# Chunk 0 of a feed-forward on one core: activations handled in TensorE's order, the down weights split earlier, and the sum T1 kept in a buffer of its own

## The reference

```python
x = x + xattn(layernorm(x), ctx, mask)       # one head, 257 context rows per batch
x = x + attn(layernorm(x), Wq, Wk, Wv, Wo)   # 16 heads of 64, causal over 32
n = layernorm(x)                             # feed-forward, hidden width 4096
x = x + (silu(n @ w_gate.T) * (n @ w_up.T)) @ w_down.T
```

## Time and profile before

| | us |
|---|---|
| median of 3 runs | 1522.84 (1522.38 to 1523.93) |
| the profiled execution | 1522.65 |
| its span | 1520.9 |
| TensorE busy | 1494.1 |
| VectorE / ScalarE / GpSimd busy | 786.9 / 539.9 / 859.4 |
| mean granted clock of TensorE | 0.996 |

### The profile page before, as it was taken

One profiled execution on the slowest core, in us unless ns is written; L12 is line 12 of the kernel. 1 busy time (PEld: TensorE's weight loads), 2 busy tenths in 40 slices (PEclk: granted clock), 3 DMA queues, 4 the chain that ended last, 5 costly groups with the idle time before them and its releaser, 6 DMA issues.

```text
span 1520.9 us, 23259 instructions
## 1 busy us (share of the span) xinstructions
PE 1494.1 (98%) x8012; PEld 1208.3 (79%) x8012; DVE 786.9 (52%) x1245; ACT 539.9 (35%) x1089; POOL 859.4 (57%) x701
## 2 busy tenths in 40 slices
PE   7999999999999999999999999999999999999998
PEld 5666788888888888778888888888888888888886
DVE  5776336154162396846436436436436446446346
ACT  3335323132132243333433433433333433433342
POOL 1111221211302221588798798798798798797795
PEclk9999999999999999999999999999999999999999
DMA  9772310100101000021121121121121121121122
GB/s 366 282 291 113 134 56 29 56 28 28 55 28 55 29 1 22 8 77 49 41 76 44 46 76 36 53 75 35 56 71 34 54 76 34 55 76 34 55 62 110
DMA packets 41798, 110.38 MB, mean 73 GB/s; under 512 B 4672, under 2 KB 4800, under 8 KB 39328
## 3 DMA queue, kind: packets, MB, share of 16 engines
q1 hardware_dynamic: 41328, 109.07, 21.0%
q10 hardware_dynamic: 432, 0.79, 0.2%
HBM read 105.65 MB, written 4.19 MB: 72 GB/s over the span
## 4 chain that ended last, share of the span: by engine, by line
PE 91%; DVE 5%; issue 1%; ACT 1%; DMA 1%; SPq 0%; DVEq 0%
PE ps L1249 37%; PE ps L1269 18%; PE ps L900 9%; PE ps L901 8%; PE ps L902 8%; PE ps L934 3%; PE ps L976 2%; PE ps L952 2%; PE ps L906 1%; DVE t_raw L1598 1%; PE ps L1050 1%; PE ps L1093 1%; DMA ctx<-in_ctx 1%; DVE x L1681 1%; DVE x L1584 1%
## 5 line engine op out<-in xcount | busy, mean ns | idle before, releaser
L536 POOL TENSOR_TENSOR b_lo<-blk,b_hi 128x512 fp32r<-128x512 f32 x180 | 239.5, 1339 | 53.2 <-ACT b_hi L795 45.0
L463 POOL TENSOR_TENSOR w_lo<-raw,w_hi 128x2048 fp32r<-128x2048 f32 x16 | 74.5, 4655 | 300.9 <-ACT w_hi L649 300.9
L1681 DVE TENSOR_TENSOR x<-ps,x 128x1024 f32<-128x1024 f32 x210 | 242.1, 1208 | 0.0
L1249 PE MATMUL ps<-xT_hi,b_hi 128*128 128x512 f32 x480 | 187.0, 390 | 2.2 <-DVE x L1584 2.2
L1249 PE MATMUL ps<-xT_hi,b_lo 128*128 128x512 f32 x480 | 186.8, 389 | 0.0
L1249 PE MATMUL ps<-xT_lo,b_hi 128*128 128x512 f32 x480 | 186.8, 389 | 0.0
L1269 PE MATMUL ps<-b_hi,b_hi 128*128 128x512 f32 x420 | 166.4, 396 | 0.0
L1269 PE MATMUL ps<-b_lo,b_hi 128*128 128x512 f32 x420 | 163.8, 390 | 0.0
L1269 PE MATMUL ps<-b_hi,b_lo 128*128 128x512 f32 x420 | 163.7, 390 | 0.0
L1655 DVE TENSOR_TENSOR hid<-ps,kept 128x512 f32<-128x512 f32 x60 | 41.5, 691 | 229.6 <-PE ps L1249 189.7
L536 POOL TENSOR_TENSOR b_lo<-s_sum,b_hi 128x512 fp32r<-128x512 f32 x105 | 138.4, 1318 | 30.5 <-ACT b_hi L795 30.5
(11 more groups left out here) (166 smaller groups left out, 3232.1 us busy)
## 6 DMA issues: line engine op xcount, KB each, us to landing
blk<-in_blocks SPq DMA_DIRECT2D x180, 256.0 KB, 2.7
ctx<-in_ctx SPq DMA_DIRECT2D x64, 512.0 KB, 8.7
raw<-in_w SPq DMA_DIRECT2D x19, 1024.0 KB, 4.9
x<-in_x SPq DMA_DIRECT2D x8, 512.0 KB, 4.8
out<-x SPq DMA_DIRECT2D x16, 256.0 KB, 2.6
xn<-in_ext ACTq DMA_DIRECT2D x3, 128.0 KB, 6.6
mask<-in_mask ACTq DMA_DIRECT2D x1, 257.0 KB, 8.4
extT<-in_ext_t ACTq DMA_DIRECT2D x1, 128.0 KB, 3.8
```

Of the source, the lines that this page charges most:

```text
L463: pool.tensor_tensor(w_lo[wslot][:, :], raw[slot][:, :], w_hi[wslot][:, :].bitcast(F32), ALU.subtract).then_inc(split_done[slot], 1)
L536: pool.tensor_tensor(b_lo[slot][:, :], src[:, :], b_hi[slot][:, :].bitcast(F32), ALU.subtract).then_inc(block_lo, 1)
L1249: mm = pe.matmul(ps[:, bank, :], stat[a], moving[b], start=first and m == 0, stop=(s == 3 and m == 2), skip_group_check=True)
L1681: dve.tensor_tensor(part, ps[:, bank:bank + 2, :], part, ALU.add).then_inc(down_added, 1)
```

## The change

Three things. On ScalarE the high part of the down weights is taken right behind that of the second gate/up weights, before the turn of token tile 6. On ScalarE and VectorE the hidden parts are handled in the order 0, 2, 1, 3 (`FIRST_HIDDEN` holds for each part its place in it, and is its own inverse), with the low part of one taken later than its product, and `down` waits for two low parts instead of three. T1 gets a buffer of its own in `raw3`, is begun before the third gate/up pair ends, and goes ahead of T2 in the order of high and low parts; the additions stand in fewer and longer pieces. The first block of chunk 1 lies on `raw3`, so ScalarE waits for T1's low part before it.

```diff
-        t1_top = sb_at("t1_top", "xT_hi1", 0, [P, K4])
-        t1_raw = sb_at("t1_raw", "xT_lo1", 0, [P, K4])
+        t1_raw = sb_at("t1_raw", "raw3", 0, [P, K4])
...
+        FIRST_HIDDEN = (0, 2, 1, 3)
...
             pair_split(NG - 1, 5)
+            weights(2, ATT_USES, 2)
             turned_hi(2, NT - 2)
...
-                act.wait_ge(gu_done, 3 if n == 1 else n + 1)
+                count = FIRST_HIDDEN.index(n) + 1
+                act.wait_ge(gu_done, count)
                 act.activation(sg(half), ps[:, 2 * n, :], ACT.Silu).then_inc(silu_done, 1)
-                act.wait_ge(h_done, n + 1)
+                act.wait_ge(h_done, count)
...
             first_hidden(0)
+            first_hidden(2)
             turned_sum_hi(1, t3_hi[:, :], raw[1][:, :])
             first_hidden(1)
-            weights(2, ATT_USES, 2)
-            first_hidden(2)
-            turned_sum_hi(2, w_hi[0][:, :], t2_raw[:, :])
             first_hidden(3)
+            turned_sum_hi(2, flat(xT_hi[1][:, 0:4, :]), t1_raw[:, :])
+            turned_sum_hi(3, w_hi[0][:, :], t2_raw[:, :])
+            act.wait_ge(t_ready, 2)
             block_high(1, 0)
             block_high(1, 1)
-            turned_sum_hi(3, flat(xT_hi[1][:, 0:4, :]), t1_raw[:, :])
+            turned_sum_hi(4, w_hi[1][:, :], t4_raw[:, :])
             act.wait_ge(split_done[2], ATT_USES + 1)
             block_high(1, 2)
             block_high(1, 3)
-            turned_sum_hi(4, w_hi[1][:, :], t4_raw[:, :])
...
-                        pe.wait_ge(h_ready, c * 4 + 3)
+                        pe.wait_ge(h_ready, c * 4 + 2)
...
-                        pe.wait_ge(h_done, c * 4 + (i // 2 + 1))
+                        pe.wait_ge(h_done, c * 4 + (FIRST_HIDDEN.index(i // 2) + 1))
...
-                dve.wait_ge(silu_done, n + 1)
+                dve.wait_ge(silu_done, FIRST_HIDDEN.index(n) + 1)
+                if n >= 2:
+                    dve.wait_ge(h_ready, FIRST_HIDDEN.index(n - 2) + 1)
                 dve.tensor_tensor(gf(half), sg(half), ps[:, 2 * n + 1, :], ALU.mult).then_inc(h_done, 1)
-                dve.wait_ge(h_hi_done, n + 1)
+
+            def first_hidden_lo(n):
+                k, half = n // 2, n % 2
+                cols = slice(half * HALF, (half + 1) * HALF)
+                dve.wait_ge(h_hi_done, FIRST_HIDDEN.index(n) + 1)
                 dve.tensor_tensor(h_lo[:, k, cols], gf(half), h_hi[:, k, cols].bitcast(F32),
                                   ALU.subtract).then_inc(h_ready, 1)
```

More of the change, by code:

```diff
@@ L1614, in _ @@
             combine(raw[0][:, :], b22[0], b12[0], ALU.subtract)
+            first_hidden_lo(0)
+            first_hidden(2)
             combine(raw[1][:, :], b22[1], b12[1], ALU.subtract)
+            first_hidden_lo(2)
             combined()
             combine(raw[1][:, :], raw[1][:, :], raw[0][:, :], ALU.add, raw=True)
-            first_hidden(1)
+            dve.wait_ge(split_done[3], ATT_USES)
+            combine(t1_raw[:, :], b12[0], b11[0], ALU.subtract)
             dve.wait_ge(gu_done, 3)
@@ L1621, in _ @@
             combine(t2_raw[:, :], raw[1][:, :], b11[0], ALU.add)
+            first_hidden(1)
+            turned_sum_lo(1, t3_lo[:, :], raw[1][:, :], t3_hi[:, :])
+            first_hidden_lo(1)
             combined()
+            combine(t1_raw[:, :], t1_raw[:, :], b12[1], ALU.add)
+            combined()
+            combine(t1_raw[:, :], t1_raw[:, :], b11[1], ALU.subtract, raw=True)
             combine(t2_raw[:, :], t2_raw[:, :], b11[1], ALU.add, raw=True)
-            first_hidden(2)
-            turned_sum_lo(1, t3_lo[:, :], raw[1][:, :], t3_hi[:, :])
             first_hidden(3)
-            combine(t1_top[:, :], b12[0], b11[0], ALU.subtract)
-            first_add(0, 2)
-            combine(t1_raw[:, :], b12[1], b11[1], ALU.subtract)
-            first_add(2, 4)
-            combined()
-            combine(t1_raw[:, :], t1_raw[:, :], t1_top[:, :], ALU.add, raw=True)
-            first_add(4, 7)
-            turned_sum_lo(3, flat(xT_lo[1][:, 0:4, :]), t1_raw[:, :], flat(xT_hi[1][:, 0:4, :]))
-            first_add(7, 10)
-            combine(t4_raw[:, :], b21[0], t2_raw[:, :], ALU.subtract)
-            first_add(10, 13)
+            dve.wait_ge(t_raw, 3)
+            combine(t4_raw[:, :], b21[0], t2_raw[:, :], ALU.subtract)
+            first_hidden_lo(3)
+            turned_sum_lo(2, flat(xT_lo[1][:, 0:4, :]), t1_raw[:, :], flat(xT_hi[1][:, 0:4, :]))
+            first_add(0, 5)
+            turned_sum_lo(3, w_lo[0][:, :], t2_raw[:, :], w_hi[0][:, :])
+            first_add(5, 10)
             combined()
             combine(t4_raw[:, :], t4_raw[:, :], b21[1], ALU.add, raw=True)
-            first_add(13, 16)
-            turned_sum_lo(2, w_lo[0][:, :], t2_raw[:, :], w_hi[0][:, :])
+            first_add(10, 16)
             turned_sum_lo(4, w_lo[1][:, :], t4_raw[:, :], w_hi[1][:, :])
```

## The result

| | before | after |
|---|---|---|
| median, us | 1522.84 (1522.29 to 1523.93, 6 runs) | 1516.88 (1515.56 to 1518.41, 6 runs) |
| profiled execution / its span | 1522.65 / 1520.9 | 1518.41 / 1516.6 |

The ratio is 0.9961, with a 95% interval of 0.9948 to 0.9974: **faster by 5.96 us**. The forecast was 7.0 saved and 1515.8. The median lies 1.1 above it and inside the range.

A forecast was written before the change was run, and what follows sets the result against it. TensorE, busy 98%, bounds the kernel; only its stalls and slow clock can be won. Stall terms of -2.92 - 1.44 - 0.71 - 0.11 - 1.77 - 0.08 = -7.0 us take the median from 1522.84 to 1515.8; range 1515.0 to 1518.6.

The forecast's parts named there:

- VectorE's queue: Chunk 0 into chunk 1: VectorE's operations timed one by one from 613.4, with all 16 additions done at 646.9.
- The split at no cost: Down weights' split moved to GpSimd at 593.2 to 597.8: taken at 0, at most 1.9 us if uncovered.
- The room ahead of place 0: Start of chunk 1: 13th addition at 645.0, TensorE needs it at 645.87, so 0.8 us of room.
- the second rival: GpSimd still runs the split across T1's sums, VectorE 4.3 later: 3.5 us lost, 1519.3; chance 0.01.
- The first rival: At the start of chunk 1 a part returns as a wait for VectorE's additions: 1516.7 to 1519.7; chance 0.09.
- the slower rival: ScalarE's `b_hi2` waits behind T4's copy in a loop through four engines: 1526.1 if 14.5 late; chance 0.04.
- The sum of the stalls: TensorE, 624 to 656: 2.92 + 1.44 + 0.71 + 0.11 + 1.77 + 0.08 = 7.03 us, all removed.
- the slow clock's term: TensorE behind the first stall, 626.98 to 630.46: nine intervals at the lower clock cost 1.44 us more.
- the ceiling of 7.03: Most the change can give, from TensorE's intervals; taken over the 7.17 by which place 1 moves.
- from 656 on the program is the same: Everything behind the turn from chunk 0 to chunk 1 is untouched, so no gain or loss there.
- The sign that I had named for it: If the stalls go and the span does not follow, something behind 656 absorbs it and the untouched-rest claim fails.

The follow-up runs named there:

- run 4: The changed kernel with the down weights' split left late: 1519.64 us, 2.8 slower than the change.
- run 6: The kernel before with one more long-met ScalarE wait ahead of the chunk loop (103 instructions): 1523.65 us, ratio 1.0007.
- run 3: The kernel before with only the hidden parts reordered, split late and T1 as before: 1521.39 us, ratio 0.9992.
- run 2: The kernel before with only the down weights' split moved ahead: 1518.28 us, ratio 0.9975.
- run 7: The kernel before with the split moved ahead and the hidden parts reordered, T1 as before: 1518.81 us, ratio 0.9975.
- run 1: The changed kernel measured a second time, unaltered: 1516.82 us, ratio 0.9964.
- run 5: The changed kernel without ScalarE's wait for `split_done[2]`, 102 instructions ahead of the loop again: 1515.23 us, ratio 0.9951.
- run 10: The changed kernel with one more long-met ScalarE wait, 104 instructions ahead of the loop: 1515.72 us, ratio 0.9951.

## Why the prediction was right, and where it was not

The forecast held in sign, in place and nearly in size. Taken step by step:

- **VectorE's queue: right.** The prediction's ends against after's rows less 1.54: T1's first subtraction starts at 609.20 (609.3), T2's first half at 613.38 (613.4), T1's second sum at 619.00 (619.1), the down matmuls at 624.06 (624.06), place 0 at 645.82 (645.87), place 1 at 648.54 (648.60). The durations came from other instances of the same shape in before.
- **The split at no cost: right.** It starts at 594.62, 1.54 earlier is 593.08, and takes 4.61; nothing waits for it.
- **The room ahead of place 0: too small.** The 13th addition ended at 643.88 + 1.88 = 645.76, 1.6 ahead of 647.36 instead of 0.8. Half of the difference was there before T2 low (additions 0 to 4 ended at 634.40, less 1.54, where I had 634.8: pitches rounded up), and GpSimd held T2 low for 0.6 (2.90 against 2.29) instead of 0.85. T4's second half wasn't held (2.28), as argued. It cost nothing here, but it mis-priced the second rival: 3.5 lost, where run 4 lost 2.8. The first rival, a wait for additions, didn't come: TensorE has no wait there in after.
- **ScalarE's queue, the slower rival: rightly small.** `b_lo2` ran from 646.50, ended at 647.79, less 1.54 is 646.25, where I had 647.1.
- **The sum of the stalls: nearly right as a total, wrong in its parts.** From 626.98 to 630.46 there are eight intervals and not nine, so the slow clock's term was 3.48 - 8 x 0.227 = 1.66 instead of 1.44, and the ceiling of 7.03 that I took as "the smaller" was 7.25. Run 6 agrees: without that term, and with 0.08 behind the stall, its down matmuls end 1.60 earlier. I also wrote the terms as if each stall had a cause of its own. Run 6 removes the slow clock's term and place 1 doesn't move; run 3 removes 2.92 + 1.66 and only 1.2 comes. All three are one chain: VectorE is late, its additions with it, and place 1 starts when they are done. The total holds because 655.77 - 648.54 = 7.23 is the distance between place 1 as VectorE's additions let it start and as TensorE's own matmuls do. So I credited the hidden order with 2.92 + 1.44 = 4.36, and the moved split with nothing of its own. The runs have it the other way round: the split alone brings 4.3 (run 2), the order alone 1.2 (run 3) and nothing on top of the split (run 7), and T1's part the last 3.1 of the stalls.
- **The step that failed: "from 656 on the program is the same", with its claim that the rest of the span isn't touched.** The text of ScalarE's loop is the same; its place in ScalarE's instructions is not. The term that was missing is 0.28 in the first down unit and about 0.10 in thirteen more, 1.5 us, of which 1.39 is left at the end. In the profiles -7.23 + 1.39 = -5.84, and the medians differ by 5.96. That the forecast was off by only 1.1 owes 0.2 to the miscounted interval, which made the forecast smaller. The sign that I had named for it, stalls gone and a span that doesn't follow, is what showed.

Open: why the start of this one ScalarE operation depends on that place. Runs 1, 5, 6 and 10 show that it does, by one instruction either way in the changed program and by one more in before; nothing in the trace shows the mechanism.

## What to carry to other kernels

Before you sum stalls, ask which engine is late at the last of them: if it is the same engine each time, only its lateness at the last customer counts, and removing an earlier stall alone returns little (here 1.2 of 4.6). Work moved out of a late engine's way pays at once; then look for what still stands between its due operations. When a loop's body has not changed, still compare its period before and after: 0.1 us in 14 passes was a fifth of this gain, and reading its cause led to one swapped pair of GpSimd operations that was worth as much as the whole change.

## What the runs showed of the hardware that I had not expected

- One met wait more ahead of ScalarE's loop moves one ScalarE start by 0.28 us in the first pass and by 0.08 to 0.09 in each other; 102 and 104 instructions give down units of 19.40, 103 gives 19.49.
- The same stall of TensorE, 3.15 from start to start, was followed by the lower clock in the profile of before and not in that of run 6. After the 3.94 of run 3 the clock fell. Before itself varies too: 3 of its 26 executions in the first set have a mean granted clock of 1.000, the others 0.995 to 0.999. So whether the clock falls behind a stall of about 3 us is not the program's alone.
- What lies ahead of chunk 0's down matmuls is nearly the same in all these kernels, and yet the last gate/up matmul started between 622.31 and 625.38 in their profiled executions. Between before and after the 1.54 arose in the first 35 us. Rows of two kernels must be aligned at an event near them before they are compared.
